# A bit-by-bit threshold search: the two vector steps behind each total become one clamp between two ready-made candidates

## The reference

```python
logits = xn @ router_weight.T + router_bias        # [8192 tokens, 16 experts]
probs = jax.nn.softmax(logits, axis=-1)
_, idx = jax.lax.top_k(logits.T, top_k)            # per expert its 512 best tokens
xe = xn[idx]
h = gelu(einsum('ecd,efd->ecf', xe, fc1_weight) + fc1_bias)
y = einsum('ecf,edf->ecd', h, fc2_weight) + fc2_bias
# gate-weighted sum of y scattered back to the tokens, divided by the sum of the gates
```

## Time and profile before

| | us |
|---|---|
| median of 3 runs | 984.46 |
| lowest and highest run | 983.14, 984.82 |
| span of the profiled execution (first to last instruction) | 983.0 |
| stretch of the search's rounds, from the span's start | 499.9 to 552.4 |
| VectorE busy in that stretch | 47.05 of 52.5 |
| GpSimd busy in that stretch | 16.91 |

### The profile page before, as it was taken

One profiled execution on the slowest core, in us unless ns is written; L12 is line 12 of the kernel. 1 busy time (PEld: TensorE's weight loads), 2 busy tenths in 40 slices (PEclk: granted clock), 3 DMA queues, 4 the chain that ended last, 5 costly groups with the idle time before them and its releaser, 6 DMA issues. The chain is left out here.

```text
span 983.0 us, 20868 instructions
## 1 busy us (share of the span) xinstructions
PE 851.7 (87%) x6067; PEld 728.5 (74%) x6067; DVE 747.5 (76%) x1660; ACT 505.7 (51%) x921; POOL 593.1 (60%) x564
## 2 busy tenths in 40 slices
PE   3899999999999999999621139999999999999995
PEld 2678878888788878887521027989999999999985
DVE  4478888888888888887388975898777778777742
ACT  1355566655665566655246205555555555555531
POOL 3246676666766676666532265588877767775344
PEclk9799999999999999999855558999999999999998
DMA  5366666665666566654232024366766665555433
GB/s 144 100 202 217 202 204 209 222 205 199 205 220 214 202 201 214 223 198 146 76 110 86 3 67 137 119 170 182 205 164 158 159 158 156 156 160 151 111 70 43
DMA packets 129540, 156.51 MB, mean 159 GB/s; under 512 B 22464, under 2 KB 104656, under 8 KB 129376
## 3 DMA queue, kind: packets, MB, share of 16 engines
q1 hardware_dynamic: 104096, 113.06, 35.6%
q0 software_dynamic: 15616, 25.70, 12.4%
q10 hardware_dynamic: 9792, 17.31, 4.8%
HBM read 74.93 MB, written 26.28 MB: 103 GB/s over the span
## 5 line engine op out<-in xcount | busy, mean ns | idle before, releaser
L575 DVE TENSOR_REDUCE NM<-bank 128x4 f32<-128x480 f32 x256 | 155.7, 650 | 65.9 <-PE bank L725 65.8
L411 ACT ACTIVATE PT<-bank 120x512 f32<-120x512 f32 x256 | 142.5, 603 | 37.1 <-PE bank L750 36.2
L348 POOL TENSOR_SCALAR XN<-X,mv,rstd 128x256 f32<-128x256 f32 x126 | 152.9, 1222 | 14.3 <-POOL rstd L343 13.5
L1632 PE MATMUL bank<-W2H,HH 128*128 128x256 f32 x512 | 144.7, 283 | 2.0 <-issue 2.0
L1634 PE MATMUL bank<-W2H,HL 128*128 128x256 f32 x512 | 143.6, 280 | 0.0
L1633 PE MATMUL bank<-W2L,HH 128*128 128x256 f32 x512 | 143.5, 280 | 0.0
L1093 POOL DMA_INDIRECT out_dram<-C,IO x60 | 110.5, 1842 | 50.6 <-issue 31.3
L1361 DVE TENSOR_TENSOR HL<-hf,HH 128x512 fp32r<-128x512 f32 x128 | 87.4, 690 | 49.9 <-ACT HH L1516 49.3
L750 PE MATMUL bank<-QX,KX 128*120 128x256 f32 x512 | 112.0, 312 | 8.5 <-DMA QX<-NMT 5.0
L533 DVE RECIPROCAL RR<-RC 128x256 f32<-128x256 f32 x64 | 111.6, 1743 | 6.8 <-DMA RC<-PVS 6.7
L341 POOL TENSOR_SCALAR ve<-mv 128x2 f32<-128x2 f32 x64 | 12.2, 191 | 163.0 <-DVE mv L523 160.4
(11 more groups left out here) (189 smaller groups left out, 1897.6 us busy)
## 6 DMA issues: line engine op xcount, KB each, us to landing
QX<-QH ACTq DMA_DIRECT2D x64, 256.0 KB
W<-w1T_dram SPq DMA_DIRECT2D x16, 1024.0 KB, 5.5
W<-w2T_dram SPq DMA_DIRECT2D x16, 1024.0 KB, 6.0
X<-x_dram SPq DMA_DIRECT2D x32, 256.0 KB, 3.1
QX<-QL SPq DMA_DIRECT2D x32, 256.0 KB
XB<-x_dram SPq DMA_DIRECT2D x32, 256.0 KB, 2.9
RC<-PVS SPq DMA_DIRECT2D x64, 128.0 KB, 2.1
OC<-PVS SPq DMA_DIRECT2D x64, 128.0 KB, 2.3
```

The source lines that it names most:

```text
L348: ins = pool.tensor_scalar(dst[:, t, :], src[:, t, :], mv[:, t, 0:1], rstd[:, t:t + 1], ALU.subtract, ALU.mult)
L411: act.activation(PT[u][0:M, HE * k:HE * (k + 1), :], score_bank(b, k // 2)[k % 2][0:M, :], ACT.Exp, scale=SCALE) \
L575: dve.tensor_reduce(NM[u][:, t, :].rearrange("p (f n e) -> p n e f", n=HN, e=HE)[:, n, :, :], smax_bank[q % 2][:, 0:4 * M].rearrange("p (e ...
L1632: pe.matmul(o, wh, xh, start=first, stop=False)
```

## The change

Behind the count VectorE now forms both possible next candidates at once, before the total is known: `nexts` (128x2) is `cand` xor the two columns of `steps` (128x2), by a TENSOR_TENSOR with both inputs in SBUF. `steps` is shifted right for the next round. TensorE's total is scaled by 2^113 (`same_big`, now bf16), and a third product adds minus the limit (`limits`), so that the total is hugely negative or positive. One TENSOR_SCALAR with max and min and two per-partition scalars, the columns of `nexts`, then picks the candidate. The sums alternate between two PSUM banks. GpSimd makes `limits` by five more MEMSETs in `search_constants`.

```diff
-            m = 3 * ROUNDS * turn + (BASE + 3 * r)
+            m = 2 * ROUNDS * turn + (BASE + 2 * r)
             own = slice(0 if alone else HT, CT)
             dve.tensor_scalar(junk[:, own], LT[:, own], cand[:, :].bitcast(FP32), None, ALU.is_ge, ALU.add,
                               accum_out=count16[:, :]).then_inc(count_ready, 1)
-            dve.tensor_scalar(bit[(r + 1) % 2][:, :], bit[r % 2][:, :], 1, None, ALU.logical_shift_right) \
+            dve.wait_ge(bit_ready, ROUNDS * turn + (r + 2))
+            dve.tensor_tensor(nexts[:, :], cand[:, :].to_broadcast([P, 2]), steps[r % 2][:, :], ALU.bitwise_xor).then_inc(step_dve, 1)
+            dve.tensor_scalar(steps[(r + 1) % 2][:, :], steps[r % 2][:, :], 1, None, ALU.logical_shift_right) \
                 .then_inc(bit_ready, 1)
-            dve.wait_ge(bit_ready, ROUNDS * turn + (r + 2))
-            dve.tensor_scalar(both[:, :], cand[:, :], bit[(r + 1) % 2][:, :], None, ALU.bitwise_xor).then_inc(step_dve, 1)
+            dve.wait_ge(step_dve, m + 1)
             dve.wait_ge(total_done, ROUNDS * turn + (r + 2))
-            dve.tensor_scalar(missed[:, :], cnt_bank[:, 0:1], GMAX if alone else SMAX, bit[r % 2][:, :], ALU.is_lt, ALU.mult) \
-                .then_inc(step_dve, 1)
+            dve.tensor_scalar(cand[:, :].bitcast(FP32), sum_bank[(r + 1) % 2][:, 0:1], nexts[:, 0:1].bitcast(FP32),
+                              nexts[:, 1:2].bitcast(FP32), ALU.max, ALU.min).then_inc(step_dve, 1)
             dve.wait_ge(step_dve, m + 2)
-            dve.tensor_scalar(cand[:, :], both[:, :], missed[:, :], None, ALU.bitwise_xor).then_inc(step_dve, 1)
-            dve.wait_ge(step_dve, m + 3)
...
-        dve.memset(bit[0][:, :], 1 << 30).then_inc(bit_ready, 1)
+        dve.memset(top_bit[:, :], 1 << 30).then_inc(bit_ready, 1)
+        dve.memset(steps[0][:, 0:1], 3 << 29)
+        dve.memset(steps[0][:, 1:2], 1 << 29).then_inc(bit_ready, 1)
...
         def total(turn, r, alone=False):
 
+            own = sum_bank[r % 2][:, 0:1]
+            v = 0 if alone else 1
+            pe.matmul(own, same_big[:, :], limits[:, v:v + 1], start=True, stop=False)
             pe.wait_ge(count_ready, ROUNDS * turn + (r + 1))
-            ins = pe.matmul(cnt_bank[:, 0:1], same_e16[:, :], count16[:, :], start=True, stop=alone)
+            ins = pe.matmul(own, same_big[:, :], count16[:, :], start=False, stop=alone)
             if not alone:
                 pe.wait_ge(signs_ready, ROUNDS * turn + (r - ALONE))
-                ins = pe.matmul(cnt_bank[:, 0:1], minus_half_e[:, :], sign16[:, :], start=False, stop=True)
+                ins = pe.matmul(own, minus_half_e[:, :], sign16[:, :], start=False, stop=True)
             ins.then_inc(total_done, 1)
...
-    pool.tensor_copy(same_e16[:, :], same_e[:, :]).then_inc(consts, 1)
+    pool.tensor_scalar(same_big[:, :], same_e[:, :], BIG, 0.0, ALU.mult, ALU.add).then_inc(consts, 1)
+    pool.memset(limits[:, :], 0.0).then_inc(consts, 1)
+    pool.wait_ge(consts, n + 3)
+    for v, limit in enumerate((GMAX, SMAX)):
+        whole = -math.copysign(math.floor(abs(limit)), limit)
+        pool.memset(limits[0:E, v:v + 1], whole).then_inc(consts, 1)
+        pool.memset(limits[2 * E:3 * E, v:v + 1], -limit - whole).then_inc(consts, 1)
+    pool.wait_ge(consts, n + 7)
```

More of the change, by code:

```diff
@@ L3 @@
 from contextlib import ExitStack
+import math
 FP32 = mybir.dt.float32
@@ L46 @@
 SMAX = GMAX - NC * HT / 2
+BIG = 2.0 ** 113
 BASE = 3
@@ L865, in _, with search_constants @@
         ins.then_inc(lt_done, 1)
-def search_constants(pool, consts, same_e, same_e_below, same_e16, zero_row):
+def search_constants(pool, consts, same_e, same_e_below, same_big, zero_row, limits):
     pool.memset(same_e[:, :], 0.0).then_inc(consts, 1)
@@ L911, in routed_phase @@
     LT, LP, odd, sign_of, _ = search_views(search_tiles)
-    same_e, same_e_below, same_e16, zero_row = search_consts
+    same_e, same_e_below, same_big, zero_row, limits = search_consts
     probs = sb("probs", [P, NT, E], FP32)
@@ L944, in routed_phase @@
     ranked2 = sb("ranked2", [P, 2, CT], FP32)
-    cand, missed, both = (sb(n, [P, 1], U32) for n in ("cand", "missed", "both"))
-    bit = [sb(f"bit{u}", [P, 1], U32) for u in range(2)]
+    cand, top_bit = sb("cand", [P, 1], U32), sb("top_bit", [P, 1], U32)
+    steps = [sb(f"steps{u}", [P, 2], U32) for u in range(2)]
+    nexts = sb("nexts", [P, 2], U32)
     missed_i, cand_i = (sb(n, [P, 1], I32) for n in ("missed_i", "cand_i"))
@@ L959, in routed_phase @@
     W1_1 = HH[1][:, :, :].rearrange("p f (s k c) -> p s k f c", s=2, k=KD)
-    minus_half_e = sb("minus_half_e", [P, P], FP16)
+    minus_half_e = sb("minus_half_e", [P, P], BF16)
     mx, rsm = gate_total, no_gate
@@ L983, in routed_phase @@
     cnt_bank, first_ends_bank = bank[2], bank[3]
+    sum_bank = bank[2:4]
     ends_bank, taken_bank, gates_bank = bank[4:6], bank[6:8], bank[6:8]
@@ L1095, in add_up @@
                     .then_inc(added, 16)
-        pool.tensor_scalar(minus_half_e[:, :], same_e16[:, :], -0.5, 0.0, ALU.mult, ALU.add).then_inc(weights_ready, 1)
+        pool.tensor_scalar(minus_half_e[:, :], same_big[:, :], -0.5, 0.0, ALU.mult, ALU.add).then_inc(weights_ready, 1)
         pool.iota(s_col[:, :], pattern=[[1, GT]], base=0, channel_multiplier=GT,
@@ L1204, in _ @@
         dve.wait_ge(total_done, 1)
-        then(dve.tensor_scalar(missed_i[:, :], cnt_bank[:, 0:1], GMAX, None, ALU.is_lt))
+        then(dve.tensor_scalar(missed_i[:, :], sum_bank[0][:, 0:1], 0.0, None, ALU.is_lt))
         then(dve.tensor_scalar(cand_i[:, :], missed_i[:, :], 31, 31, ALU.logical_shift_left, ALU.arith_shift_right))
         dve.wait_ge(bit_ready, 1)
-        then(dve.tensor_scalar(cand[:, :], cand_i[:, :].bitcast(U32), bit[0][:, :], None, ALU.bitwise_xor))
+        then(dve.tensor_scalar(cand[:, :], cand_i[:, :].bitcast(U32), top_bit[:, :], None, ALU.bitwise_xor))
@@ L1215, in _ @@
         decide(0, 30, True)
-        n[0] = BASE + 3 * 31
+        n[0] = BASE + 2 * 31
         dve.wait_ge(sum_ready, 4)
@@ L1531, in signs @@
         def signs(r):
-            act.wait_ge(step_dve, BASE + 3 * r)
+            act.wait_ge(step_dve, BASE + 2 * r)
             with nc.allow_low_precision(reason="a whole number of at most 512"):
@@ L1742, in program @@
         search_consts = [ctx.enter_context(nc.sbuf_tensor(name, shape, dt)) for name, shape, dt in
-                         (("same_e", [P, P], FP32), ("same_e_below", [P, P], FP32), ("same_e16", [P, P], FP16),
-                          ("zero_row", [P, CT], FP32))]
+                         (("same_e", [P, P], FP32), ("same_e_below", [P, P], FP32), ("same_big", [P, P], BF16),
+                          ("zero_row", [P, CT], FP32), ("limits", [P, 2], FP16))]
         search_tiles = [ctx.enter_context(nc.sbuf_tensor(name, shape, FP32)) for name, shape in
```

## The result

Over 20 runs each the changed kernel took 988.44 us (median; 984.68 to 991.61) and the kernel before 984.59 (981.96 to 987.24). The ratio, taken over all the runs and not from the two medians, is 1.0041, with a 95% interval of 1.0032 to 1.005: 3.2 to 4.9 us slower. The profiled run took 988.26, with a span of 986.5 us where it was 983.0.

A forecast was written before the change was run, and what follows sets the result against it. VectorE's chain of search rounds was taken as the bound: -6.0 (clamp) + 0.6 (MEMSETs) + 10.8 (waits for GpSimd) = +5.4 us, forecast 989.9; own range 985.5 to 993.7, widened to 981.0 to 994.0.

The forecast's parts named there:

- A: Search: nexts, with two SBUF inputs, waits for GpSimd's whole instruction; 989.9 us, chance 0.77.
- the clamp in place of two steps: Round's tail: one clamp replaces missed and cand, 0.195 us less over 31 rounds, 6.0 us in all.
- the exclusion: Search: VectorE's two-SBUF-input nexts and GpSimd's SBUF reads keep each other out; 10.8 us lost, 8.5 to 12.5.
- start of the search (MEMSETs): GpSimd's constants ahead of the search: five added MEMSETs and a wait delay its start by 0.6 us, 0.35 to 0.9.
- The clamp's price: Search round: the one-element clamp with two per-partition scalars takes 277 ns, bounds 220 and 340.
- The gain: Search: the shorter tail of each round saves 6.0 us over 31 rounds, bounds 4.2 and 7.9.
- It starts where `missed` does: Round's tail: the clamp starts when missed did, 0.03 us behind the second product's end, since nexts should be done.
- rival D: Round's tail: a third wait makes the clamp no shorter than the pair; only losses, +0.6 to +11 us; chance 0.03.
- The loss: Search rounds beside GpSimd: 3.7 us for each of two long instructions, 2.7 second expert, 0.7 softmax sums; 10.8 in all.
- So the added MEMSETs delay the search one for one: Attention phase's end: TensorE's projection waits for GpSimd, so the added MEMSETs' 0.6 us reaches the search in full.
- B: Search: nexts does not wait for GpSimd, so the kernel is faster, -5.4 us to 979.1; chance 0.13.
- C: Search: nexts waits only 0.3 to 0.7 us per meeting with GpSimd; -2.9 us, 981.6; chance 0.07.

The follow-up runs named there:

- both repairs: Changed kernel with steps moved to PSUM and the wait for nexts moved from the clamp to the shift: median 977.36 us, ratio 0.9906 to the kernel before.
- the second input's run: Kernel before, with only `both` formed by a TENSOR_TENSOR of two one-element SBUF tiles instead of a TENSOR_SCALAR: 992.78 us, beside 984.34.

## Why the prediction was right

The forecast was 989.9 us, 5.4 above the kernel before; 988.44 was measured, 3.85 above it and in its own range of 985.5 to 993.7. The case came true by name: A, `nexts` waits for GpSimd's whole instruction. The sum of its terms, against the 3.5 us of the profile:

| term, us | forecast | measured | from |
|---|---|---|---|
| the clamp in place of two steps | -6.0 | -3.70 | steps in PSUM, against before |
| the exclusion | +10.8 | +8.70 | after, against steps in PSUM |
| the search, together | +4.8 | +5.00 | |
| start of the search (MEMSETs) | +0.6 | +0.14 | start of the first round |
| everything behind the search | 0 | -1.64 | |
| span | +5.4 | +3.5 | |

**The clamp's price** of 277 ns, put together from 60 ns for each per-partition scalar, was 276 to 279. **The gain** was oversized by 2.3 us. The step "It starts where `missed` does" failed by 0.08: with two waits on it the clamp starts 0.30 behind the second product's start, with one 0.22. The run with both repairs has the round that was forecast, and gains 5.67 us. The prediction had seen a further wait on the clamp as rival D, but put nothing in its sum for one that is long satisfied.

**The loss** was oversized by 2.1 us, in three places. The two long rounds took 4.64 us (511.88 to 516.52) and 4.80 (522.47 to 527.27), against 1.48 to 1.51, so 3.2 and 3.3 lost, not 3.7. The prediction let GpSimd's instruction begin at the round's start; it began 0.23 and 0.07 ahead of it. And it put 0.61 us between the end of GpSimd's instruction and the next count: 516.52 - 516.15 = 0.37 it was, since `nexts` ends 0.02 behind GpSimd and not a whole 0.15, the shift starts before `nexts` has ended, and the clamp before the shift has. The second expert's two rounds took 2.62 and 2.30, so 1.1 and 0.8, together 1.9 where 2.7 was forecast. The softmax sums met one `nexts`, for 0.5 us, of which the round lost some 0.25, with the forecast at 0.7. 3.2 + 3.3 + 1.9 + 0.25 = 8.65, which is the 8.70 of the comparison. That the wait lasts for the whole of GpSimd's instruction was right, but the prediction's own rows did not show it: the CAST of the earlier trace rows ended at 650.07, 0.54 us before the issue that it was said to wait for (650.61). It was the second input's run that showed it.

**The MEMSETs** cost GpSimd 0.77 us where 0.6 was forecast: they follow one another at 0.15 us, not 0.10, and the last wait is 0.22. But the step "So the added MEMSETs delay the search one for one" did not hold in general. The projection is on the path, but its duration goes with the clock that TensorE is granted there, from 1.99 to 3.78 us, and what decides on that clock is open. With the MEMSETs alone the profile has the forecast delay, 0.75 us; in the changed kernel's the projection began 1.87 us later and took 1.66 less, so that 0.14 was left; in the eight profiles that have the MEMSETs it is 0.1 to 2.7. The timed runs with them alone leave everything from -2.8 to +1.2 us open.

**Behind the search** the prediction let everything move by as much. It was 1.64 us shorter. The stretch in which the experts' products begin shows a difference in the clock, before and after (both begin 22.7 us behind the end of the last `cand`, to 0.1; columns as above):

```profile
575.00:600.00 25.00, 16.29 (x66) 0.71 0.50 143
```

```profile
580.10:605.10 25.00, 15.61 (x65) 0.75 0.51 148
```

The granted clock was 0.75 where it was 0.71, and TensorE was busy for 0.68 us less. What follows the search was between 429.1 and 432.7 us in the profiles of all the versions, none of which changes an instruction of the experts' products, so I take it as the kernel's scatter and not as an effect of the change, which no run tests by itself. It is also why the medians of 20 runs, 3.85 apart, are the number to trust, not one pair of spans. This scatter happened to offset a part of the loss in the profile. That the forecast of the search came within 0.2 us is luck as well: gain and loss were oversized by nearly the same, 2.3 and 2.1.

**The rivals.** B fell in the trace, with blocks of 3.62 and 3.77 us. C fell with them, since a block lasts to the end of GpSimd's instruction, not for a piece. D's mechanism is real at 0.08 us a round and not enough to make the clamp as long as the pair.

## What to carry to other kernels

- Before giving VectorE a small instruction inside a chain, look at what GpSimd does beside it. Two SBUF tensor inputs, or one at two elements a partition, can make 0.15 us into nearly the length of GpSimd's instruction; here `steps` in PSUM, or instructions with one tensor input and one element, avoided it. The median duration doesn't show it: look at the maximum of the group.
- A wait that is satisfied long ago still cost 0.08 us a round on the instruction whose release sets the end: put it on an instruction before it that has slack, and check what that one can collide with.
- Where TensorE's granted clock goes between 0.50 and 1.00 on the path, a shift of under a microsecond ahead of it does not arrive one for one: bound it by the steps behind at both clocks.

## What the runs showed of the hardware that was not expected

- The exclusion acts at one element for two inputs (158 to 3477 ns), and for one input at two elements a partition (224 to 3782) but not at one (208 to 210), with all 128 partitions in each. `steps` in PSUM ended it (150 to 152).
- The shift with one SBUF input collided with GpSimd's MEMSETs too (0.84 us of one of 1.80), which two inputs did not.
- The second wait on the clamp cost 0.08 us, though what it waited for had ended 0.35 us earlier; moving it took the undisturbed round from 1.48 to 1.40 or 1.41 in both pairs of runs that differ by it.
- Between two GpSimd instructions on end VectorE gets in: `nexts` and the shift right behind it, in the changed kernel. The shift that a wait held until 0.03 us behind the end of `nexts` was shut out for 2.27.
- Of the attention phase's last projection, the same eight matmuls took 1.99 us at a granted clock of 1.00 and 3.78 at 0.50, and what stands between it and the search 12.5 to 12.7 or 14.0.
